# Cross-attention block with an MLP on one core: bias adds, weight splits and normalisations in another order, large buffers at multiples of 128 bytes

## What is computed

```python
xq  = layer_norm(x, qn_w, qn_b)                 # x: 2 x 2048 x 512
ctx = layer_norm(context, cn_w, cn_b)           # context: 2 x 77 x 512
q = (xq @ q_w).reshape(B, N, H, D)              # 16 heads of 32
k, v = split(ctx @ kv_w)
attn = softmax(where(xa_mask, -FLT_MAX, q @ k.T * D ** -0.5))
x = x + (attn @ v) @ proj_w + proj_b
h = layer_norm(x, n2_w, n2_b)
out = x + gelu(h @ fc1_w + fc1_b) @ fc2_w + fc2_b   # hidden size 2048
```

## Time and profile before

| | before |
|---|---|
| median of 3 runs | 1096.28 us (1095.53 to 1099.5) |
| the profiled execution | 1097.95 us, span 1096.2 us |
| PE busy | 1068.0 us (97%) |
| DVE busy | 836.1 us (76%) |
| ACT busy | 463.1 us (42%) |
| POOL busy | 354.5 us (32%) |
| mean granted clock of TensorE | 0.995 |
| chain that ended last | PE 76%, DVE 13%, DMA 5%, issue 3%, POOL 2%, ACT 1% |

### The profile page before, as it was taken

One profiled execution on the slowest core, in us unless ns is written; L12 is line 12 of the kernel. 1 busy time (PEld: TensorE's weight loads), 2 busy tenths in 40 slices (PEclk: granted clock), 3 DMA queues, 4 the chain that ended last, 5 costly groups with the idle time before them and its releaser, 6 DMA issues.

```text
span 1096.2 us, 16339 instructions
## 1 busy us (share of the span) xinstructions
PE 1068.0 (97%) x5793; PEld 866.9 (79%) x5793; DVE 836.1 (76%) x1355; ACT 463.1 (42%) x830; POOL 354.5 (32%) x257
## 2 busy tenths in 40 slices
PE   8999999999999998999999999999999999999998
PEld 6788888877788776878778888888888888888887
DVE  7888889998988788778787766677766668656555
ACT  4355354555454764445452433352343344223221
POOL 2556555656578645222613100301300120400000
PEclk9999999999999999999999999999999999999999
DMA  7012112111111063745376535244734523834312
GB/s 255 1 40 68 49 69 78 70 59 60 59 59 41 20 231 135 269 177 178 125 292 219 228 125 228 109 173 159 261 137 154 190 105 138 305 133 168 113 75 77
DMA packets 49607, 148.84 MB, mean 136 GB/s; under 512 B 8131, under 2 KB 16363, under 8 KB 41349
## 3 DMA queue, kind: packets, MB, share of 16 engines
q1 hardware_dynamic: 48957, 146.93, 36.9%
q10 hardware_dynamic: 584, 1.06, 0.3%
HBM read 108.13 MB, written 39.85 MB: 135 GB/s over the span
## 4 chain that ended last, share of the span: by engine, by line
PE 76%; DVE 13%; DMA 5%; issue 3%; POOL 2%; ACT 1%; ACTq 0%; DVEq 0%; POOLq 0%
PE bank L1743 29%; PE bank L1713 26%; PE bank L1586 7%; PE bank L1543 4%; PE bank L1555 3%; DMA xr<-in_x 3%; PE bank L1524 2%; DVE xhat L1158 2%; DMA x_scratch<-xr 2%; PE bank L1572 2%; DVE hring L1324 1%; DVE nmax L1111 1%; PE bank L1722 1%; DVE aTl L1130 1%; DVE esum L1135 1%
## 5 line engine op out<-in xcount | busy, mean ns | idle before, releaser
L1743 PE MATMUL bank<-w2r,gT 128*128 128x512 f32 x1536 | 365.6, 395 | 3.3 <-DVE acc L1348 3.2
L1743 PEld LDWEIGHTS bank<-w2r,gT 128*128 128x128 f32 x1536 | 287.7, 188 | 69.7 <-DVE acc L1348 5.3
L1713 PE MATMUL bank<-hop,w1r 128*128 128x512 f32 x1344 | 321.9, 397 | 1.2 <-POOL w2r L728 1.2
L1713 PEld LDWEIGHTS bank<-hop,w1r 128*128 128x128 f32 x1344 | 252.4, 189 | 62.4 <-issue 2.1
L1348 DVE TENSOR_TENSOR acc<-bank,acc 128x512 f32<-128x512 f32 x256 | 176.8, 691 | 108.3 <-PE bank L1743 102.0
L1335 DVE TENSOR_TENSOR ybuf<-bank,ybuf 128x512 f32<-128x512 f32 x224 | 147.7, 687 | 84.4 <-PE bank L1713 78.9
L987 ACT ACTIVATE ybuf<-ybuf,cols 128x512 f32<-128x512 f32 x128 | 91.7, 716 | 172.1 <-DVE ybuf L1335 172.1
L826 ACT ACTIVATE PT<-bank 77x512 f32<-77x512 f32 x128 | 68.9, 590 | 75.8 <-PE bank L1555 74.4
L633 POOL TENSOR_TENSOR S<-S,rsum 128x1232 f32<-128x1232 f32 x32 | 72.4, 2261 | 74.8 <-DVE rsum L1140 74.8
L1340 DVE TENSOR_TENSOR gT<-ybuf,gT 128x512 fp32r<-128x512 f32 x128 | 96.1, 772 | 0.0
L598 POOL TENSOR_TENSOR hrs<-hve,mhalf 128x1 f32<-128x1 f32 x32 | 18.0, 561 | 235.2 <-DVE hve L1320 235.2
(11 more groups left out here) (107 smaller groups left out, 1447.7 us busy)
## 6 DMA issues: line engine op xcount, KB each, us to landing
w1r<-w_scratch SPq DMA_DIRECT2D x24, 1792.0 KB, 7.3
w2r<-w_scratch SPq DMA_DIRECT2D x24, 1024.0 KB, 5.1
w_scratch<-w1r SPq DMA_DIRECT2D x8, 1792.0 KB, 5.8
xr<-in_x SPq DMA_DIRECT2D x16, 512.0 KB, 4.0
x_scratch<-xr SPq DMA_DIRECT2D x16, 512.0 KB, 2.8
hring<-x_scratch SPq DMA_DIRECT2D x32, 256.0 KB, 2.8
acc<-x_scratch SPq DMA_DIRECT2D x32, 256.0 KB, 4.1
w_scratch<-w2r SPq DMA_DIRECT2D x8, 1024.0 KB, 8.8
```

The costliest lines, as they stand in the source:

```text
L1713: mm = pe.matmul(bank_[:, :], w1r[:, w1_slot(s), c, w, kk * P:(kk + 1) * P], hop[i][:, d, kk, :], start=(kk == 0 and n == 0), stop=(kk == ...
L1743: mm = pe.matmul(bY[t % 2][:, :], gT[s % 2][:, j, d, t * P:(t + 1) * P], w2r[:, s % 2, j, w, :], start=(n == 0), stop=(n == 5))
```

## The change

Five edits, with no instruction added or taken away:

- The large buffers (1024 bytes per partition or more) start at a multiple of 128 bytes, and `S1`, `PT`, `S0` too, so that `wp`, `aT`, `gT0`, `w1r`, `xr`, the accumulators, `raw`, `T`, `hring` and `ybuf` move to such places.
- VectorE, attention: `exp_sum(0)` and `recip(0)` come before `av_lo(1)` and `h_normed`, and the second half of `normed` comes after `av_lo(3)`.
- GpSimd, attention: `acc_bias` comes after `probs(1)`.
- Block 0 of the MLP: ScalarE makes `w1_hi(s+1, 0)` and `w1_hi(s+1, 1)` before `m1_copy(s)`, where they came after gelu 0; in set 1, GpSimd's three `acc_bias` come after the first `h_rstd`.
- All blocks: VectorE's second `h_normed` of a set comes before `w1_lo(s+1, 3)` and `acc_add` 6, where it came after them.

```diff
--- before.py
+++ after.py
@@ -122,8 +122,9 @@
         for s in shape[1:]:
             size *= s
         if offset is None:
-            offset = top[0]
-            top[0] += (size + 31) // 32 * 32
+            grain = 128 if size >= 1024 else 32
+            offset = (top[0] + grain - 1) // grain * grain
+            top[0] = offset + (size + 31) // 32 * 32
         return nc.alloc_sbuf_tensor_at(name, shape, dt, offset=offset)
 
 
@@ -146,10 +147,13 @@
     vtok = at("vtok", [P, B, C], F32)
     qrow = at("qrow", [1, C], F32, offset=top[0])
     aT = [at(f"aT{s}", [P, KT, UN], F32R) for s in "hl"]
+    top[0] = (top[0] + 127) // 128 * 128
     S1_at = top[0]
     S1 = at("S1", [P, UT, H * M], F32)
+    top[0] = (top[0] + 127) // 128 * 128
     PT_at = top[0]
     PT = at("PT", [P, H, UN], F32)
+    top[0] = (top[0] + 127) // 128 * 128
     S0_at = top[0]
     S0 = at("S0", [P, UT, H * M], F32)
     xr_at = S0_at + 2 * 7 * 4 * P * 4 - 2 * UT * C * 4
@@ -163,6 +167,7 @@
     mv = at("mv", [P, UT, 2], F32)
     veps = at("veps", [P, UT], F32)
     rstd = at("rstd", [P, UT], F32)
+    assert xr_at % 128 == 0 and S0_at % 128 == 0 and PT_at % 128 == 0
     acc = [at(f"acc{t}", [P, C], F32) for t in range(BT - 3)]
     acc.append(at(f"acc{BT - 3}", [P, C], F32, offset=projb_at))
     acc += [at(f"acc{BT - 2 + i}", [P, C], F32, offset=xr_at + (2 * UT + i) * C * 4) for i in range(2)]
@@ -678,12 +683,12 @@
             if late:
                 add_projb(k, 0)
                 add_projb(k, 1)
-            if bias is not None:
-                acc_bias(0, bias)
             if scores:
                 less_max(1)
                 probs(0)
                 probs(1)
+            if bias is not None:
+                acc_bias(0, bias)
             if tail == 1:
                 add_projb(last_unit, 0)
                 add_projb(last_unit, 1)
@@ -743,17 +748,17 @@
                     hop_T(b + 1, range(4))
                 if first and 0 < s < SETS - 1:
                     w1_sums(s + 1)
-                if first and s == 1:
-                    for t in range(BT - 3, BT):
-                        acc_bias(b, t)
                 if first and s == 0:
                     w2_lo(s)
                 if s == 0 and not first:
                     for t in range(BT):
                         acc_bias(b, t)
                 if not last:
-                    for t in TILES.get(s, ()):
+                    for n, t in enumerate(TILES.get(s, ())):
                         h_rstd(b + 1, t)
+                        if first and s == 1 and n == 0:
+                            for i in range(BT - 3, BT):
+                                acc_bias(b, i)
                 if first and s > 0:
                     w2_lo(s)
 
@@ -996,6 +1001,9 @@
             for s in range(SETS):
                 refill = not last and s == SETS - 1
                 made = first and 0 < s < SETS - 1
+                if made:
+                    w1_hi(s + 1, 0)
+                    w1_hi(s + 1, 1)
                 if first and s == 0:
                     t_proj.wait(act, last_unit, UT - 1)
                 else:
@@ -1009,9 +1017,6 @@
                 if refill:
                     for i in range(1, 4):
                         hop_hi(b + 1, i)
-                if made:
-                    w1_hi(s + 1, 0)
-                    w1_hi(s + 1, 1)
                 gelu(b, s, 1)
                 gelu(b, s, 2)
                 gelu(b, s, 3)
@@ -1151,9 +1156,9 @@
                 v_mv.wait(dve, n, UT - 1)
                 dve.tensor_scalar(veps[:, :], mv[:, :, 1], EPS, None, ALU.add).then_inc(v_veps.sem, 1)
 
-            def normed():
+            def normed(tiles=range(UT)):
                 p_rstd.wait(dve, n, 0)
-                for t in range(UT):
+                for t in tiles:
                     t_xT.wait(dve, n.plus(-1), t)
                     dve.tensor_scalar(xhat[:, t:t + 1, :], xr[:, bass.ds(n.slot(), 1), t, :], mv[:, t, 0:1],
                                       rstd[:, t:t + 1], ALU.subtract, ALU.mult).then_inc(v_xhat.sem, 1)
@@ -1256,21 +1261,25 @@
                 y_add(0, 0, C11)
             if front:
                 q_lo(0)
-            if norm2 is not None:
-                h_normed(0, norm2)
-            if back:
+            if tail == 1:
                 av_lo(1)
             if scores:
                 exp_sum(0)
                 recip(0)
+            if norm2 is not None:
+                h_normed(0, norm2)
+            if back and tail != 1:
+                av_lo(1)
             if tail == 2:
                 hop_lo(0, 4)
             if back:
                 av_lo(2)
             if norm:
-                normed()
+                normed((0,))
             if back:
                 av_lo(3)
+            if norm:
+                normed((1,))
             if front:
                 q_lo(1)
             if tail == 2:
@@ -1436,11 +1445,11 @@
                 if made:
                     w1_lo(s + 1, 2)
                 add(s, 5)
+                if len(tiles) > 1:
+                    h_normed(b + 1, tiles[1])
                 if made:
                     w1_lo(s + 1, 3)
                 add(s, 6)
-                if len(tiles) > 1:
-                    h_normed(b + 1, tiles[1])
                 add(s, 7)
             if last:
                 for t in range(BT):
```

## The result

The changed kernel takes 1067.64 us (median of 4 runs, 1066.52 to 1068.94), the kernel before 1097.89 us in 4 runs beside it (1095.53 to 1101.86): a ratio of 0.9721, with a 95% interval of 0.9688 to 0.9755. The forecast was 1068.4 us, so it was right, within its own range of 1064 to 1073. The profiled execution took 1067.7 us with a span of 1065.9, against 1097.95 and 1096.2 before.

What follows compares the result with a forecast made beforehand. TensorE was taken as the bound: matmul pace in the MLP, waits in the attention and block 0. Terms -13.2 - 5.6 - 3.7 - 5.0 - 1.5 + 1.1 = -27.9 us from 1096.28 gave 1068.4 us, range 1064 to 1073.

Steps and rivals of the forecast that it cites:

- Edit 1: Buffer starts at multiples of 128 bytes: faster `mul` and even-set fc2 in the MLP, -13.2 us, bounds 0 and -14.8.
- the 1.1 us waited out: Sets 1, 3, 5 and block 0's end: faster `mul` gains 0.28 us each, lost to remaining VectorE waits, +1.1 us.
- the case for which the prediction named 14.8 us: Bound of the buffer-start term: both kinds of fc2 sets settle at 226.7 ns, -14.8 us.
- Edit 2: VectorE and GpSimd order in attention steps 4 to 11: TensorE's `av_lo` waits go, -5.6 us, between -6.0 and 0.
- The `av_lo(1)` that I feared: Attention: `av_lo(1)` next in line to be late for `av(3)`; 0.4 us set aside.
- Edit 3: Block 0, set 1, `w1_hi` early and `acc_bias` later: `acc_add` wait 3.2 to about 1.3 us; -3.7 us, bounds -1.9 and -5.0.
- the clock's 1.8 us: Block 0, set 1: clock expected to hold after the shortened `acc_add` wait, 1.8 us of the -3.7 us term.
- Edit 4: Second `h_normed` earlier in sets 1, 3, 5: `hring` waits shorter, -5.0 us, clock holds, -1.5 us; bounds -2.5 and -7.4.
- Rival 1: MLP matmuls: the start of buffers doesn't matter, that term and the 1.1 us go; 1080.5 us, chance 0.19.
- Rival 2: Attention: GpSimd's `probs(0)` starts first behind the reciprocal, `h_normed` waits 2.25 us, -5.6 becomes +5; 1079 us, chance 0.08.
- Rival 3: Stalls move on (DMA landings, ScalarE's order): edits 2 to 4 bring 6 us instead of 15.8; 1078 us, chance 0.06.
- Rival 4: Attention: `h_normed`'s 2.25 us wait reaches TensorE whole and the clock falls, 4.05 us in 8 steps; 1106.4 us, chance 0.03.

Runs made afterwards that it cites:

- off128_256: Changed kernel with `gT0` and `w1r` 128 bytes further up and `gT1` 256 bytes further up: 1078.81 us (one run).
- attn_only: Kernel before with only the new attention order on VectorE and GpSimd: 1089.86 us, ratio 0.9930.
- pool_first: Changed kernel with `h_normed` behind `av_lo(1)` in the attention, so GpSimd's `probs(0)` starts ahead of it: 1074.90 us (one run).
- no_align: Changed kernel with the starts of the buffers as in the kernel before: 1079.54 us, ratio to the kernel before 0.9836.
- align_only: Kernel before with only the large buffers' starts at multiples of 128 bytes: 1083.54 us, ratio 0.9873.
- accbias_only: Kernel before with only set 1's three `acc_bias` moved behind the first `h_rstd`: 1097.07 us (one run).
- improved: Changed kernel; in block 0 GpSimd's `w2_lo` waits for the set's last `w1_lo`, and set 1's `w1_sums` follows the first `h_rstd`: 1062.32 us, ratio to before 0.9685.
- tiles_only: Kernel before with only VectorE's second `h_normed` moved ahead of `w1_lo` 3 and `acc_add` 6: 1090.54 us (one run).

## Why the prediction was right

**Edit 1: right, for a reason that was half right.** Forecast -12.1 us with the 1.1 us waited out; measured 11.9 (without it in the changed kernel) to 13.5 us (alone). Both kinds of fc2 sets did settle at 226.7 ns, the case for which the prediction named 14.8 us. Some of that is lost again: behind transposes 24 products of fc2 take 5.49 us and not 5.44. The rest was not followed up. The step from odd and even sets to the distance between two operands held. Its number, 128 bytes, did not: the period is 256, and had `gT0` and `w1r` landed the other way, as in `off128_256`, the time would have been 1078.8 us (one run). The fast kernel is in this part luck. The Trainium skill, "SBUF — State Buffer", section "Who interferes with whom", names no other contention in SBUF than that for the port pair which VectorE and GpSimd share. By it this term would be 0 and the time 1080.5 us; the measurement decides against that. It speaks of engines in each other's way, and what the paces show goes with the starts of TensorE's own two operands.

**Edit 2: the mechanism right, the term mis-sized.** The prediction priced it by the idle time, 5.6 us; the stage gave 7.7 us, `attn_only` 8.0 us. The step that was mis-sized is to take the idle time of a wait for its cost. Here are the starts on either side of the wait of the earlier trace rows, in the kernel before (TensorE, projection):

```profile
249.17 0.39 PE L1586 MATMUL bank<-wph,aTl 128*128 128x512 f32 x1
...
250.49 0.39 PE L1586 MATMUL bank<-wpl,aTh 128*128 128x512 f32 x1
```

From 249.17 to the start of the waiting matmul at 250.15 are 0.98 us, and the next one comes 0.34 us later, where two starts are 0.227 us apart elsewhere. That is 0.87 us lost beside 0.60 us of idle time, 0.27 us more: 0.16 us because a product's row lasts 0.39 us while the next may start 0.227 us behind it, and 0.11 us because the second start is late. The waits of the earlier trace rows and an eighth of 0.15 us, too short for that list, show the same 0.27 to 0.28 us each, together 2.1 us, which is what was missing. It is not the chance of one profile: steps 4 to 11 less their idle time take 181.1 to 181.5 us in the five profiles with the old order, and 179.2 to 179.4 us in the nine with the new one. It does not hold everywhere: in `pool_first`, six waits in front of transposes, 5.2 us of idle time, made steps 4 to 11 longer by 4.7 us, 0.6 us of other waits gone. The `av_lo(1)` that I feared was late for `av(3)` by 0.2 us in three steps (0.6 us in the waits), near the 0.4 us set aside. The order behind the reciprocal came out as worked out from the starts 0.17 and 0.33 us behind it.

**Edit 3: right in place, with a wait in its wake that the prediction did not see.** The wait fell to 1.09 us (forecast 1.3), and the clock's 1.8 us came back. But `g_lo` 1 of sets 2, 4 and 6 came to stand beside `w2_lo`, 2.2 us of waits in all. So edits 3 and 4 brought 8.0 us in block 0 (`no_align` against before; 7.4 us by the changed kernel against `align_only`) where 10.2 were forecast. I had worked out the meeting with `acc_bias` in set 1 and not gone through the next set. `accbias_only` shows the same meeting from a smaller shift, and `improved`, which moves `w2_lo` away from it, gives it back.

**Edit 4: right.** Three waits of 0.41 to 0.44 us instead of 2.0 us; `tiles_only` brought 5.8 us of 6.5 alone.

**The clock.** Over block 0 the granted clock is 1.00 in the changed kernel and 0.98 in the kernel before, where it fell to 0.50 after the waits of 3.2 us and, at 483, of 2.0 us. A wait of 2.0 us does not always do it: set 1's does not in the kernel before, and does in `accbias_only`; set 3's does in the kernel before, and does not in `attn_only`. What else decides is open.

**The sum.** The span shrank by 30.3 us where 27.9 were forecast, and it came this near because misses cancel. Edit 2 brought 2.1 us more than forecast and the stage of block 0 2.5 us less, and 1.9 us of the 30.3 lie in the first stage, where the change has no part. Without them the profiles give -28.4 us beside the -27.9 forecast.

**The rivals.** Rival 1 (no effect of starts) is refuted by `align_only`. Rival 2's meeting is real, but its order did not occur. Made on purpose it costs up to 7.2 us in one run (4.7 us of it in steps 4 to 11), where I had put 10.6; and TensorE waits in front of the transposes of `hring`, not of `av(3)`, because `pool_first` leaves `av_lo(1)` ahead. So the price of the rival as I wrote it was not measured. `h_normed` takes 0.45 us in front of `probs(0)` and 2.42 us behind it. The section of the Trainium skill named above says that whichever of the two engines issues first gets the shared pair for its whole instruction and the other is blocked. The trace agrees for a VectorE instruction that comes second; `probs(0)`, when it comes second, takes 2.40 us instead of 2.25, with 0.29 us of `h_normed` left to wait for. Rival 3 was true in a small part (2.2 us of new waits). Rival 4 needed rival 2's wait to reach TensorE whole in every step and the clock to fall; in `pool_first` the waits are at most 1.5 us, and in the 140 us from 240 on the granted clock is 1.00.

## What to carry to other kernels

When the same matmul runs at two paces, compare the start addresses of the operand that stays and the one that streams: here a distance that is a multiple of 256 bytes gave 226.7 ns a product, others up to 234.2, 12 us of 1097 for an edit of the allocator. Writing the 256 into the allocator, which was not run, would no longer leave it to luck. Price a wait of TensorE by the starts around it and not by its idle time. And when an order of VectorE or GpSimd is shortened in one set, go through the next set for instructions that now start beside each other: a VectorE instruction that started just behind a GpSimd one took 2.4 us instead of 0.5 (`h_normed`) and 2.6 to 2.9 us instead of 0.7 (`g_lo`), while GpSimd, starting second behind the short `h_normed`, lost 0.15 us.

## What the runs showed of the hardware that I had not expected

- The pace of 128x512 products depends on the distance modulo 256 bytes between the starts of their two operands in SBUF: 226.7 ns at 0 (227.5 in the odd sets of the kernel before), 228.8 at 192, 232.4 at 128, 233.3 to 233.4 at 64, 160 and 224, 234.2 at 96.
- A wait of 0.60 us idle time cost the projection 0.87 us, and all eight such waits cost 0.27 to 0.28 us more than their idle time.
- The granted clock stood at 0.50 for most of the 12 products behind 1.79 us of idle time, as behind 3.22 us, and the same wait of 2.0 us left it at 1.00 in one kernel and not in another.
